# Quantizing the first gate and up weight block inside the h2 pass, and an earlier-written residual load in the down projection

## The reference

```python
def _quant_weight(w):
    scale = jnp.mean(jnp.abs(w)) + EPS
    wq = jnp.clip(jnp.round(w / scale), -1.0, 1.0)
    return (wq, scale)
def _quant_act(x):
    s = jnp.max(jnp.abs(x), axis=-1, keepdims=True) / 127.0 + EPS
    xq = jnp.clip(jnp.round(x / s), -128.0, 127.0)
    return (xq, s)
def _qlinear(x, w):
    wq, ws = _quant_weight(w)
    xq, xs = _quant_act(x)
    return jnp.einsum('bsi,oi->bso', xq, wq) * xs * ws
gate = silu(_qlinear(h, w_gate)); up = _qlinear(h, w_up)
x = x + gb * _qlinear(gate * up, w_down)
```

## Time and profile before

| | us |
|---|---|
| median of 2 runs | 7534.75 |
| profiled execution, device time | 7533.31 |
| its span, core 0 (the slowest) | 7531.8 |
| spans of the other seven cores | 7464.7 to 7513.6 |
| p5 on core 0, from its first transpose to the last tile's store | 3476.9 to 3792.7 |
| p6 on core 0, from TensorE's first matmul to its last | 3903.9 to 5826.1 |

### The profile page before, as it was taken

The page is one execution under the profiler, slowest core; times in us unless marked ns, Lnnn a source line. Parts: engine busy times, 40 slices in busy tenths (PEclk is TensorE's granted clock), DMA queues, the critical chain, the costliest instruction groups (busy, mean ns, idle before and its releaser), DMA issues.

```text
span 7531.8 us, 62909 instructions; the slowest of 8 cores (7464.7 to 7531.8 us)
## 1 busy us (share of the span) xinstructions
PE 4718.6 (63%) x20620; PEld 2111.9 (28%) x21006; DVE 3245.5 (43%) x4780; ACT 622.4 (8%) x923; POOL 488.0 (6%) x400
## 2 busy tenths in 40 slices
PE   3441389999933334461029999999998056474739
PEld 1130134444412221120014444444444022132314
DVE  0036544335515542434346666666664424141511
ACT  0001000110053330000000000000000000000000
POOL 1100000000000000000000000100000001010101
PEclk6555699999955556675569999999999578687869
DMA  8933578788733325232245555555553445555544
GB/s 118 136 81 134 141 189 212 195 225 233 212 93 100 93 65 112 80 112 63 76 96 143 142 140 141 139 137 143 140 139 102 146 142 179 154 180 144 188 139 146
DMA packets 884566, 1044.55 MB, mean 139 GB/s; under 512 B 564722, under 2 KB 744963, under 8 KB 859667
## 3 DMA queue, kind: packets, MB, share of 16 engines
q0 software_dynamic: 179408, 436.36, 26.4%
q1 hardware_dynamic: 682756, 386.03, 18.3%
q10 hardware_dynamic: 22080, 218.11, 8.5%
HBM read 881.08 MB, written 209.72 MB: 145 GB/s over the span
## 4 chain that ended last, share of the span: by engine, by line
PE 32%; DVE 28%; DMA 20%; SPq 7%; issue 6%; ACT 3%; another core or an unknown queue 3%; DVEq 1%; ACTq 0%; POOLq 0%; POOL 0%
PE ps L492 13%; PE ps L1494 8%; SPq L98 6%; DMA wf<-wuT 5%; DMA wmbuf<-wmod 4%; DMA wf<-wgT 3%; PE ps L994 3%; PE ps L1324 2%; DVE tf32c L1298 2%; DVE i32c L1301 2%; PE ps L1333 2%; DMA gut<-sp_gu 2%; DVE tf32g L1404 2%; DVE gut L1409 2%
## 5 line engine op out<-in xcount | busy, mean ns | idle before, releaser
L1324 PE MATMUL ps<-wqgbf,h2qfm 128*128 128x512 bf16 x4014 | 953.2, 389 | 586.4 <-DVE wqubf L1303 581.7
L1494 PE MATMUL ps<-guqf,wdb 128*128 128x512 bf16 x4014 | 918.9, 390 | 543.3 <-DMA guqf<-sp_guq 386.4
L1333 PE MATMUL ps<-wqubf,h2qfm 128*128 128x512 bf16 x4014 | 919.9, 379 | 6.3 <-DVE gub L1351 2.0
L492 PE MATMUL ps<-h_all,wbuf 128*128 128x512 bf16 x3010 | 675.8, 384 | 140.3 <-DMA wbuf<-wq 92.7
L1324 PEld LDWEIGHTS ps<-wqgbf,h2qfm 128*128 128x128 bf16 x4096 | 408.0, 100 | 1095.2 <-issue 635.5
L1494 PEld LDWEIGHTS ps<-guqf,wdb 128*128 128x128 bf16 x4096 | 408.8, 100 | 1054.3 <-issue 595.9
L1333 PEld LDWEIGHTS ps<-wqubf,h2qfm 128*128 128x128 bf16 x4096 | 400.6, 98 | 485.7 <-issue 2.9
L1175 DVE TENSOR_REDUCE acc<-wsb 128x1 f32<-128x4096 f32 x96 | 424.3, 4420 | 203.1 <-DMA wsb<-wuT 162.9
L492 PE MATMUL ps<-wbuf,h_all 128*128 128x512 bf16 x2007 | 442.5, 380 | 11.9 <-DVE stg L508 9.6
L492 PEld LDWEIGHTS ps<-h_all,wbuf 128*128 128x128 bf16 x3072 | 302.2, 99 | 514.5 <-issue 169.7
L1504 DVE TENSOR_TENSOR t<-ps,xsb 128x512 f32<-128x512 f32 x64 | 44.3, 692 | 911.2 <-PE ps L1494 908.7
(11 more groups left out here) (184 smaller groups left out, 3654.5 us busy)
## 6 DMA issues: line engine op xcount, KB each, us to landing
wdb<-sp_wqd POOLq DMA_DIRECT2D x64, 2048.0 KB, 13.0
wsb<-wgT ACTq DMA_DIRECT2D x32, 2048.0 KB, 10.6
wsb<-wuT ACTq DMA_DIRECT2D x32, 2048.0 KB, 10.0
wsb<-wdT ACTq DMA_DIRECT2D x32, 2048.0 KB, 9.9
wf<-wgT POOLq DMA_DIRECT2D x64, 1024.0 KB, 8.7
wf<-wuT POOLq DMA_DIRECT2D x64, 1024.0 KB, 8.4
wdf<-wdT POOLq DMA_DIRECT2D x64, 1024.0 KB, 12.2
wmbuf<-wmod POOLq DMA_DIRECT2D x48, 1024.0 KB, 11.1
```

What stands on the lines that cost most here:

```text
L492: d("tensor", lambda e, lhsT=lhsT, rhs=rhs, k=k, bank=bank: e.matmul(ps[bank][:, 0:512], lhsT, rhs, start=(k == 0), stop=(k == ND - 1)), " ...
L1324: d("tensor", lambda e, k=k, tt=tt, gbank=gbank, icsl=icsl: e.matmul(ps[gbank][:, 0:512], h2qfm[:, k * T + 128 * tt:k * T + 128 * (tt + 1) ...
L1333: d("tensor", lambda e, k=k, tt=tt, ubank=ubank, icsl=icsl: e.matmul(ps[ubank][:, 0:512], h2qfm[:, k * T + 128 * tt:k * T + 128 * (tt + 1) ...
L1494: d("tensor", lambda e, ic=ic, msl=msl, bank=bank: e.matmul(ps[bank][:, 0:512], wdb[:, msl * NIC * 128 + 128 * ic:msl * NIC * 128 + 128 * ...
```

## The change

The three large weight buffers and `emit_piece` move out of p6 into a new `make_p6pre`, whose generator is advanced once at the end of every token tile of p5. Step k (0 to 15) emits piece k of block 0, as long as k is below 8, and the two `sgcol` columns of tile k; `gmax` is cleared ahead of p5's first tile. p6 then starts with its loop. ScalarE's silu now waits for the value of VectorE's count at which its column was written. In p78 the issue of the residual load stands ahead of SP's and ACT's waits for the segment's transposes in the source, and ACT is given copies of those waits behind it.

```diff
@@ p5, at the end of the loop over tt @@
                     kb.guards[("h2qfm", j)] = list(fb_last.values())
+                kb.tick6(1)
             kb.guards[("h2qfm",)] = list(fb_last.values())
...
+        def make_p6pre(E):
+            wf32 = E(nc.sbuf_tensor("wf32", [128, 2048], F32))
+            wqgbf = E(nc.sbuf_tensor("wqgbf", [128, 2 * ND * 512], BF16))
+            wqubf = E(nc.sbuf_tensor("wqubf", [128, 2 * ND * 512], BF16))
+            vq_ic = {}
+            v_sg = {}
...
+            def gen():
+                d("vector", lambda e: e.memset(gmax[:, :], 0.0), "V")
+                yield
+                for k in range(NT):
+                    if k < 8:
+                        vq_ic[0] = emit_piece(0, k)
+                    d("vector", lambda e, k=k: e.tensor_tensor(
+                        sgcol[:, k:k + 1], s_all[:, k:k + 1],
+                        wsum[:, 4:5], OP.mult), "V")
+                    d("vector", lambda e, k=k: e.tensor_tensor(
+                        sgcol[:, NT + k:NT + k + 1], s_all[:, k:k + 1],
+                        wsum[:, 5:6], OP.mult), "V")
+                    v_sg[k] = kb.cnt["V"]
+                    yield
...
@@ p6 @@
-            kb.wait("vector", "V", kb.cnt["V"])
-            d("vector", lambda e: e.memset(gmax[:, :], 0.0), "V")
-            for tt in range(NT):
-                d("vector", lambda e, tt=tt: e.tensor_tensor(
-                    sgcol[:, tt:tt + 1], s_all[:, tt:tt + 1],
-                    wsum[:, 4:5], OP.mult), "V")
...
-            vq_ic = {}
-            for pidx in range(8):
-                vq_ic[0] = emit_piece(0, pidx)
             for ic in range(NI):
...
                     kb.wait("scalar", "T", vtg)
+                    kb.wait("scalar", "V", v_sg[tt])
@@ p78, per segment @@
             for seg in range(NQ):
+                kb.guard_wait("scalar", ("x1qb",))
+                vx1 = kb.dma("scalar", x1qb[:, :].rearrange("p (m t) -> p m t", t=512),
+                             hap(sp_x1, 512 * seg, [[T, 128], [128 * T, ND], [1, 512]]),
+                             "x1q")
                 kb.dwait("sync", xs2dma[seg])
+                kb.dwait("scalar", xs2dma[seg])
                 for v_ in sp7[seg].values():
                     kb.dwait("sync", v_)
+                    kb.dwait("scalar", v_)
                 kb.guard_wait("sync", ("guqf",))
+                kb.guard_wait("scalar", ("guqf",))
...
-                kb.guard_wait("scalar", ("x1qb",))
-                vx1 = kb.dma("scalar", x1qb[:, :].rearrange("p (m t) -> p m t", t=512),
...
```

More of the change, by code:

```diff
@@ L1256, in p65_gen @@
                 yield
[L1258 to L1271, removed]
-            kb.wait("vector", "V", kb.cnt["V"])
-            d("vector", lambda e: e.memset(gmax[:, :], 0.0), "V")
-            for tt in range(NT):
-                d("vector", lambda e, tt=tt: e.tensor_tensor(
-                    sgcol[:, tt:tt + 1], s_all[:, tt:tt + 1],
-                    wsum[:, 4:5], OP.mult), "V")
-                d("vector", lambda e, tt=tt: e.tensor_tensor(
-                    sgcol[:, NT + tt:NT + tt + 1], s_all[:, tt:tt + 1],
-                    wsum[:, 5:6], OP.mult), "V")
+        def make_p6pre(E):
[4 more added lines that the diff above has]
+            v_sg = {}
             def emit_piece(ic, pidx):
@@ L1300, in emit_piece @@
                         wsr1[wsel][:, :], MAGIC, OP.mult, OP.add), "V")
-                    vq0 = d("vector", lambda e: e.tensor_scalar(
+                    d("vector", lambda e: e.tensor_scalar(
                         i32c[:, :], tf32c[:, :], -MAGIC, None, OP.add), "V")
@@ L1310, in emit_piece, with p6, tick65 @@
                 return vq
-            vq_ic = {}
-            for pidx in range(8):
-                vq_ic[0] = emit_piece(0, pidx)
+            def gen():
[12 more added lines that the diff above has]
+                    yield
+            return gen(), emit_piece, vq_ic, v_sg, wqgbf, wqubf
+        def p6(E6, h2qfm, p6x):
+            emit_piece, vq_ic, v_sg, wqgbf, wqubf = p6x
+            sgb = E6(nc.sbuf_tensor("sgb", [128, 2 * 512], BF16))
+            gub = E6(nc.sbuf_tensor("gub", [128, 2 * 512], BF16))
+            mx2 = E6(nc.sbuf_tensor("mx2", [128, 2], F32))
+            g65 = p65_gen(E6)
+            next(g65)
+            def tick65(n=1):
+                for _ in range(n):
+                    if next(g65, "END") == "END":
+                        return
             for ic in range(NI):
@@ L1465, in p78 @@
                                              f"gq{ic % 4}", transpose=True)
-                kb.guard_wait("scalar", ("x1qb",))
-                vx1 = kb.dma("scalar", x1qb[:, :].rearrange("p (m t) -> p m t", t=512),
-                             hap(sp_x1, 512 * seg, [[T, 128], [128 * T, ND], [1, 512]]),
-                             "x1q")
                 kb.wait("tensor", "V", xs2v[seg])
@@ L1560, in build_nc, with tick6 @@
                 h2qfm = s56.enter_context(nc.sbuf_tensor("h2qfm", [128, ND * T], BF16))
+                g6pre, ep6, vq6, vsg6, wqg6, wqu6 = make_p6pre(s56.enter_context)
+                next(g6pre)
+                def tick6(n=1):
+                    for _ in range(n):
+                        if next(g6pre, "END") == "END":
+                            return
+                kb.tick6 = tick6
                 p5(s56.enter_context, h2qfm)
+                for _ in range(NT):
+                    if next(g6pre, "END") == "END":
+                        break
                 if kb.dump:
@@ L1566, in build_nc @@
                 with ExitStack() as s6:
-                    p6(s6.enter_context, h2qfm)
+                    p6(s6.enter_context, h2qfm, (ep6, vq6, vsg6, wqg6, wqu6))
                 kb.barrier()
```

## The result

| | before | changed |
|---|---|---|
| median of all runs of the comparison, us | 7618.64 (12 runs) | 7570.44 (13 runs) |
| lowest run, us | 7533.31 | 7434.86 |
| profiled execution, us | 7533.31 | 7434.86 |
| its span, and core | 7531.8, core 0 | 7433.3, core 7 |
| median of its eight cores' spans | 7502.3 | 7415.8 |

The ratio of changed to before is 0.9867, 95% interval [0.983, 0.9904]: 1.3% faster, the forecast being 0.9886. A second measurement of the changed kernel gave 0.9861 [0.982, 0.9901].

The account below looks back on a forecast made before the run. The prediction took p6 to be bound by its chain of weight pieces through one load buffer. Starting it inside p5 wins 102.8 us, less 18 of p5 growth: 84.8 off 7533.3, forecast 7449 us, range 7430 to 7480.

Parts of the forecast that it names:

- What bounds: p6 is a chain of weight pieces through one load buffer; TensorE waits, so the chain's start time can be won.
- E: The moment SP issues the last token tile's store in p5; TensorE's block 1 forecast at E + 128.1 instead of E + 230.9.
- VectorE's side of the pieces: In p5, 5.3 us of piece and `sgcol` work per tile fits VectorE's 7.57 us hole, costing nothing.
- The DMA side: In p5, loads beside transposes cost 12 us at two batches and 6 at six tiles: 18 us, ends 5 and 46.
- The new wait at product 2: In p6, VectorE's product 2 waits for product 0's store behind SP's batch of transposes, until E + 32.0.
- TensorE off the path: TensorE finishes block 0 at about E + 115, 13 us ahead of block 1's pieces, so it does not bound.
- p78 and everything else: The residual load edit in p78, silu's new wait and everything from block 1 on: worth 0.
- rival 1: In p5, load overlap costs nothing at tiles and the small end at batches: 5 us growth, 7435 us; chance 0.12.
- Rival 2: In p5, six tiles each grow 5.2 us and the two batches by 15: 46 us growth, 7476 us; chance 0.14.
- rival 3: In p5, transposes and loads exclude each other, costing 141 us against 102.8 won: 7571 us, slower; chance 0.03.
- Rival 4: In p6, TensorE stays at its low clock through block 0, losing 64 us again: about 7512 us; chance 0.03.
- Rival 5: The eighth piece is not what held TensorE at p6's start, so nothing moves: 7533 us; chance 0.02.

Follow-up runs that it names:

- two-buffer run: Changed kernel with two buffers instead of one for the loaded weight piece (`wf32`); profiled run 7332.4 us.
- spaced pieces: Changed kernel with the eight pieces behind token tiles 0, 1, 2, 4, 5, 6, 8, 9, so no load runs beside batches behind tiles 3 and 7; 7440.8 us.
- all three edits: Changed kernel with pieces behind other tiles, block 0's first four product stores from ScalarE and two weight-load buffers; 0.9664 of the kernel before, lowest run 7290.9 us.
- stores from ScalarE: Changed kernel with the first four product stores of block 0 issued by ScalarE instead of SP; E to block 1 112.4 us.

## Why the prediction was right in its steps and wrong in its number

**What bounds.** Right. The pieces held TensorE; moved, they gave back 105.1 us between E and block 1, against 102.8, and the two-buffer run shows that they were also what a block of p6 waited for.

**VectorE's side of the pieces: nothing.** Right, and shown from both sides: two more instructions were free, six more were not.

**The DMA side: 12 us for the batches, 6 for the tiles.** Right in kind. The batches cost 2.6 and 7.2 us instead of 4 and 8, since core 0, on whose 5.0 us half of my price rested, was the dearest of the eight. Taking the loads away won 8.6. That leaves 4 to 5 us for the tiles, against 6; no run isolates them. The Trainium skill's rule (page DMA: Bandwidth & Descriptors, section "Issuing engines are not separate DMA queues"), by which the three loads would have cost 22.5 us beside the batches, is borne out in that the price is not zero; the measured one is 2.6 + 7.2 = 9.8 us, under half of it, and the measurement decides.

**The new wait at product 2.** Right in place and releaser. It came at E + 28.0 instead of E + 32.0, because the batch took 23.1 us on this core, not 25.7, and the store landed within 2.1 instead of 2.9. These 4 us are most of the difference to E + 128.1.

**TensorE off the path.** Right: done at E + 114 (I had E + 115), and holding it changed nothing that shows.

**p78 and everything else: 0.** Right for the edit. What I did not price is that the untouched stretches scatter by 10 us and more between runs.

**The number.** Here the prediction failed: 7430 to 7480 was given, and the median over the 13 runs is 7570.44. The step that failed is the one that set the profiled execution's time beside "the median of the runs" and took 7449 for both, with 5 and 4 us at the ends of the range for what differs from run to run. The two runs of before that I had, 7533.3 and 7536.2, are the two lowest of the 12 of the comparison, whose median of 7618.64 is 84 us higher, as much as the whole gain that was forecast; the changed kernel's median lies 136 us above its profiled execution. Nothing in the working allowed for that; the range held only what the change itself left open. The ratio, 0.9886 by the forecast, lies inside both measured intervals.

Two agreements are luck. The profiled execution, 7434.86, has the time of rival 1, whose step was wrong: with the measured stretches the sum is 7533.3 - 91.3 = 7442.0, and the other 7 us lie in stretches that the change leaves alone and in another core being the slowest. And the middle one of the five runs listed with the result, 7450.7, lies 2 us from the forecast 7449 because two errors cancel: the base of 7533.3 was 22 us below the mean of 7555.8, and the gain of 84.8 us was 15 short of the 100 by which the two means differ. Of these 15 us the two stretches show 6.5; the rest can't be told from scatter.

**The rivals.** Rival 1 (the overlap is free) falls by the spaced pieces. Rival 2 (full collisions) and rival 3 (exclusion) fall by tiles of 15 to 18 us (17.6 at most, in the first profile of the changed kernel). Rival 4 (a low clock through block 0) falls by the timeline of TensorE: one slow group behind each long hole. Rival 5 (nothing moves) falls by the 105.1 us.

## What to carry to other kernels

An engine that idles for a fixed time in every turn of a serial loop is a place for work of the next stage, up to the length of that hole; read the hole and its releaser from the rows, and look at what the moved work's transfers then run beside. When the head of a chain is moved forward, ask what stands in the DMA issuer's list between the old and the new place: here a small store behind 16 transposes kept 11 us of the gain. And if a chain of load and use goes through one buffer, a second buffer may be worth more than the earlier start: 15 blocks at some 9 us here, against 91 us for the whole change. Last, two runs that lie within 3 us of each other do not give the median of a kernel's runs: here they were the two lowest of twelve, and a forecast that is added to them should be given as a ratio, or with a range that holds the scatter.

## What the runs showed of the hardware that I had not expected

A load of 1 MB beside a batch of 16 transposes lengthens SP's issue of the batch by 2 to 5 us, not by the load's 7.5, and two loads by 7.2; the price on one core was twice that on another with the same work. In the kernel with all three edits the batch behind tile 15 took from 23.7 us on core 0 to 37.8 on core 2.

TensorE's slow start is not tied to a long rest. In the changed kernel the first group took 5.48 us behind a hole of 9.30 us, and in the kernel with all three edits, on core 4, 6.50 us behind one of 3.03 us, as much as the 6.23 behind one of 92.79; the granted clock from 3847.4 to 3850.0 us, right behind the 3.03 us, was 0.50. Behind 1.51 us the group took 3.61, and so it did behind a hole of 3.11 us on core 7 of the kernel with stores from ScalarE, so the length of the hole alone does not decide it. In the kernel with two buffers such holes are gone from block to block, and its blocks of 111.1 us are 32 groups at 3.45 us and less than 1 us more.
